# Attention softmax over heads: the layout of the exponentials, the form of their sums and the share of GpSimd are changed

## The chip, the core and the metric

The kernel runs on one core of a Trainium2 chip. The metric is the time of the whole kernel on the device, in microseconds. Before the change the median of 3 runs is 1029.59 us (1028.51 to 1030.99).

## The reference

A gated block of cross attention and a quantised feed-forward net, for 8 sequences of 512 tokens of width 256. Only the attention is touched by the change. Cut to that:

```python
q = (query @ Wq + bq).reshape(Bq, Sq, H, DK)      # Bq = 8, Sq = Sk = 512, H = 16, DK = 16
k = (key @ Wk + bk).reshape(Bq, Sk, H, DK)
v = (value @ Wv + bv).reshape(Bq, Sk, H, DK)
scores = jnp.einsum('bqhd,bkhd->hbqk', q, k) / np.sqrt(DK)
attn = jax.nn.softmax(scores.reshape(H * Bq, Sq, Sk), axis=0).reshape(H, Bq, Sq, Sk)
out = jnp.einsum('hbqk,bkhd->bqhd', attn, v).reshape(Bq, Sq, H * DK)
```

The softmax runs over axis 0, which is heads and batch together: for each pair of a query position and a key position, the 16 x 8 = 128 exponentials of all heads and all sequences are summed, and each is divided by that sum. So no product with v can be scaled afterwards by one factor a query: each exponential is multiplied by its own reciprocal before it meets v.

## The kernel before

Four stages follow each other: `prepare` (projections, stacks of q and k in DRAM), `maxima` (the maximum over heads and batch, `shift`), `attend`, and `ffn`. The change touches `attend` alone.

`attend` runs over 4 query chunks of 128 (`qc`) and for each over 64 steps: 4 key chunks (`kc`) times 16 heads (`h`). A step makes the 128 keys x (8 sequences x 128 queries) exponentials of one head, CT = 1024 for each of the 128 partitions, and stores them in one slot of the ring `e`, as 8 blocks of 128 queries, one for each sequence. 16 steps of one key chunk share one sum. The engines work as follows.

- SyncE loads k for the step four ahead (L653), and for the last 16 steps of a query chunk also q of the next chunk; at step `LAG + 2` of the next chunk it stores the finished sums of the last one (L592, eight transfers), ahead of the further k loads in its queue.
- TensorE (program L683 and on) makes the scores of a step in two halves, each into its own bank `ps` (`shift` subtracted by L694, then four products, L698). The first half of the next step waits for ScalarE to have read the same bank (`exped`). Then it multiplies the scaled exponentials of the step 20 back (`LAG`) with v: `times_v`, L716, eight f32 products with 32 columns each, four column groups of the array side by side, accumulated in `acc` (each is recorded as two instructions). This waits for `pool_scaled` and `dve_scaled` of that step.
- ScalarE takes exp of each half from `ps` into the slot (L763, 512 elements). It waits for the slot to be multiplied already. After each query chunk it copies `acc` out (`gather`, L754), and TensorE waits for that before it clears `acc`.
- VectorE first scales the step 17 back (`SLAG`, L798), the last 2 or 3 of its 8 blocks, with the reciprocals in PSUM (`recip_v`); then it adds the step's two halves to `total`, 512 columns in PSUM (L819 or, for the first head, a copy at L821; then L823). Each add waits for the one before it (`sum_done`). After the 16th head it folds 4 blocks into 128 sums (L826, a reduce over a step of 128 elements), takes the reciprocal into `recip` (L832) and copies it into PSUM (L834).
- GpSimd scales the first 6 or, in one step of 4, 5 blocks of each slot with `recip` (L786). It waits only for `recip_ready`, once in 16 steps. In the very last 16 steps its share is 3 and 2 blocks.

The ring has 21 slots and an extra one for the last step of a query chunk. After the last step, 17 scales of VectorE and 20 `times_v` remain.

Of the kernel before, what the change touches and what calls it, by code (L numbers as in the profile page):

```python
# [595 lines left out]
def attend(nc, sem, k_stack, q_stack, out_parts, ffn_small, x_first, keep):  # L596
# [14 lines left out]
    RING = 21  # L611

    def slot(i):

        i %= STEPS
        return RING if i == STEPS - 1 else i % RING

    def pool_share(i, ending):

        if ending and i >= STEPS - H:  # L620
            return 3 if i < STEPS - H // 2 else 2
        return 6 if i % 4 else 5

    with ExitStack() as es:
        def sb(name, shape, dt=F32):
            return es.enter_context(nc.sbuf_tensor(name, shape, dt))

        e = sb("e", [P, RING + 1, CT])
# [5 lines left out]
        total = es.enter_context(nc.psum_tensor("total", [P, BANK], F32))  # L634
# [5 lines left out]
                                       "recip_copied", "pool_scaled", "dve_scaled", "multiplied", "gathered"))  # L640

        with nc.Block() as block:
# [40 lines left out]
            def _(pe):  # L683
# [22 lines left out]
                def times_v(done, i, half):  # L706

                    kc, h = i // H, i % H
                    if half == 0:
                        pe.wait_ge(pool_scaled, done)  # L710
                        pe.wait_ge(dve_scaled, done)
                    for b in range(half * HB, (half + 1) * HB):
# [4 lines left out]
                                                e[:, slot(i), b * P:(b + 1) * P], start=False, stop=False,  # L717
# [13 lines left out]
                def chunk(qc, first):  # L731
                    for i in range(STEPS):
# [7 lines left out]
                        if i >= LAG or not first:  # L740
                            for half in range(2):
                                times_v(qc * STEPS + (i - LAG + 1), (i - LAG) % STEPS, half)
# [3 lines left out]
                for i in range(STEPS - LAG, STEPS):  # L746
                    for half in range(2):
                        times_v((NC - 1) * STEPS + i + 1, i, half)

            @block.scalar  # L750
            def _(act):
# [4 lines left out]
                def chunk(qc, first):  # L756
                    for i in range(STEPS):
# [3 lines left out]
                        for half in range(2):  # L761
                            act.wait_ge(scored, qc * (2 * STEPS) + (2 * i + half + 1))
                            nc.scalar.activation(e[:, slot(i), half * BANK:(half + 1) * BANK], ps[half][:], ACT.Exp,  # L763
                                                 scale=DK ** -0.5).then_inc(exped, 1)
# [10 lines left out]
            def _(pool):  # L775
# [3 lines left out]
                def chunk(qc, ending):  # L779
                    for i in range(STEPS):  # L780
                        kc = i // H
                        if i % H == 0:
                            pool.wait_ge(recip_ready, qc * NC + (kc + 1))
                        share = pool_share(i, ending)
                        part = e[:, slot(i), 0:share * P].rearrange("p (b q) -> p b q", q=P)
                        nc.gpsimd.tensor_tensor(part, part, recip[:, kc % 2, :].rearrange("p (a q) -> p a q", a=1)  # L786
                                                .to_broadcast([P, share, P]), ALU.mult).then_inc(pool_scaled, 1)
# [5 lines left out]
            def _(dve):  # L793
                def scale(i, ending=False):
                    kc = (i // H) % NC
                    share = pool_share(i % STEPS, ending)
# [585 lines left out]
```

## Time and profile before

| | us |
|---|---|
| median of 3 runs | 1029.59 |
| the profiled execution | 1029.23 |
| its span, first to last instruction | 1027.3 |
| VectorE busy | 897.1 (87%) |
| TensorE busy | 797.8 (78%) |
| ScalarE busy | 645.1 (63%) |
| GpSimd busy | 519.2 (51%) |
| first and last exponential start | 357.5 and 819.7 |

The profile is one execution on the chip. PE is TensorE (PEld its weight loads), DVE is VectorE, ACT is ScalarE, POOL is GpSimd, SP is SyncE; L12 is line 12 of the kernel. A group or a timeline row names engine, line, operation, and output <- inputs. Behind a row stands the idle time of the engine just before it, and what released it. In a timeline, instructions that follow each other closely are merged into one piece, which carries the shape of only one of them; their starts tell the pace better than their durations, since neighbours overlap. The granted clock PEclk is a share of TensorE's full 2.4 GHz.

### The profile page before, as it was taken

To read this page: it belongs to the slowest core of one execution; us is meant where nothing else is said; L and a number is where in the kernel's file an instruction comes from. 1 tells how busy PE (TensorE), PEld (TensorE's weight loads), DVE (VectorE), ACT (ScalarE), POOL (GpSimd) and SP (SyncE) were. 2 spreads that over 40 slices of the span, in tenths; PEclk is the share of its full clock that TensorE was granted. 3 is DMA by queue.
4 is the path that set the end of the run, shared out by engine and by line. 5 is a ranking of instruction groups with operands and counts; after the bars stand their busy time and mean duration, and the time that the engine had idled before them with its cause. 6 is when DMAs were issued, how large, how long until landed. Compare 5 with 4: busy or idle time off the path is not lost. (4 is left out here: it accounts for less than half of the span.)

```text
span 1027.3 us, 21516 instructions
## 1 busy us (share of the span) xinstructions
PE 797.8 (78%) x8175; PEld 445.5 (43%) x8184; DVE 897.1 (87%) x1428; ACT 645.1 (63%) x981; POOL 519.2 (51%) x330
## 2 busy tenths in 40 slices
PE   2798883777777689989888998988889869067656
PEld 1455540111111145555555655655556548022223
DVE  3679843999999889999989999999989978868968
ACT  3354562999999776655655656655656502567673
POOL 4132330000000009999989999999989976022300
PEclk9898896999999899999999999999999979589979
DMA  9489897455445665586556846576465446000013
GB/s 283 164 266 347 262 332 266 164 196 210 167 176 209 229 185 153 145 265 183 148 168 192 279 143 170 158 233 215 138 176 164 129 171 190 0 1 1 0 42 123
DMA packets 112396, 180.94 MB, mean 176 GB/s; under 512 B 10032, under 2 KB 37296, under 8 KB 112304
## 3 DMA queue, kind: packets, MB, share of 16 engines
q1 hardware_dynamic: 112304, 179.67, 55.0%
q8 instruction: 63, 1.03, 0.4%
q14 instruction: 29, 0.24, 0.1%
HBM read 137.70 MB, written 41.94 MB: 175 GB/s over the span
## 5 line engine op out<-in xcount | busy, mean ns | idle before, releaser
L786 POOL TENSOR_TENSOR e<-e,recip 128x768 f32<-128x768 f32 (+3 forms) x256 | 424.7, 1712 | 59.8 <-DVE recip L832 59.8
L763 ACT ACTIVATE e<-ps_att 128x512 f32<-128x512 f32 x512 | 279.6, 595 | 172.4 <-PE ps_att L698 171.9
L694 PE MATMUL ps_att<-shift,minus 128*128 128x512 bf16 x512 | 201.6, 394 | 20.3 <-DMA arena<-k_stack 8.9
L698 PE MATMUL ps_att<-arena 128*128 128x128 bf16 x2048 | 203.4, 223 | 0.0
L716 PE MATMUL acc<-e,arena 128*32 128x128 f32 x4096 | 170.6, 285 | 37.9 <-DVE e L798 33.8
L553 ACT ACTIVATE copies<-ps_max 128x1024 bf16<-128x1024 f32 x192 | 179.0, 1031 | 20.9 <-PE ps_max L533 20.9
L698 PEld LDWEIGHTS ps_att<-arena 128*128 128x128 bf16 x2048 | 161.6, 100 | 64.0 <-issue 6.0
L823 DVE TENSOR_TENSOR total<-total,e 128x512 f32<-128x512 f32 x256 | 178.9, 699 | 8.7
L533 PE MATMUL ps_max<-q_head,k_head 128*128 128x512 bf16 x512 | 138.4, 386 | 60.7 <-DVE high L572 21.5
L819 DVE TENSOR_TENSOR total<-total,e 128x512 f32<-128x512 f32 x240 | 166.3, 693 | 2.1 <-ACT e L763 0.7
L716 PEld LDWEIGHTS acc<-e,arena 128*32 128x32 f32 x4096 | 105.2, 111 | 74.5 <-issue 54.0
L798 DVE TENSOR_TENSOR e<-e,recip_v 128x256 f32<-128x256 f32 (+3 forms) x256 | 119.0, 470 | 4.2 <-ACT e L763 4.2
L577 DVE TENSOR_TENSOR high<-copies,high 128x3072 bf16<-128x3072 bf16 x64 | 111.6, 1744 | 0.0
L533 PEld LDWEIGHTS ps_max<-q_head,k_head 128*128 128x128 bf16 x512 | 34.8, 97 | 164.0 <-ACT copies L553 72.6
L50 POOL MEMSET minus<- 128x128 bf16 x1 | 0.2, 206 | 204.1 <-POOLq L498 204.1
L572 DVE TENSOR_TENSOR high<-ps_max,high 128x1024 bf16<-128x1024 f32 x64 | 77.6, 1212 | 7.5 <-PE ps_max L533 7.5
L191 POOL TENSOR_TENSOR parts<-rest,parts 128x512 bf16<-128x512 f32 x32 | 37.2, 1163 | 91.1 <-ACT parts L321 91.1
L694 PEld LDWEIGHTS ps_att<-shift,minus 128*128 128x128 bf16 x512 | 50.1, 98 | 72.4 <-issue 54.6
L455 DVE TENSOR_TENSOR rest<-full,parts 128x512 f32<-128x512 f32 x32 | 32.8, 1023 | 27.1 <-ACT parts L347 27.1
L216 PE MATMUL psT<-ident,arena 128*128 128x128 f32 x128 | 23.4, 323 | 32.2 <-POOL ident L52 12.3
L1180 POOL TENSOR_TENSOR arena<-up,sil 128x512 f32<-128x512 f32 x16 | 21.6, 1350 | 50.8 <-ACT up L1114 50.8
L1285 PE MATMUL psD<-wd_T,hq 128*128 128x256 bf16 x192 | 30.0, 288 | 20.6 <-DVE hq L1263 20.6
(129 smaller groups left out, 850.8 us busy)
## 6 DMA issues: line engine op xcount, KB each, us to landing
arena<-k_stack SPq DMA_DIRECT2D x256, 256.0 KB, 2.9
k_stack<-parts SPq DMA_DIRECT2D x64, 256.0 KB, 3.8
q_stack<-parts SPq DMA_DIRECT2D x64, 256.0 KB, 3.7
k_head<-k_stack SPq DMA_DIRECT2D x16, 1024.0 KB, 5.6
q_head<-q_stack SPq DMA_DIRECT2D x16, 1024.0 KB, 7.8
arena<-q_stack SPq DMA_DIRECT2D x64, 256.0 KB, 4.4
arena<-in_x_dram SPq DMA_DIRECT2D x5, 1024.0 KB, 7.8
arena<-in_ctx_dram SPq DMA_DIRECT2D x4, 1024.0 KB, 6.9
```

Of the source, the lines that this page charges most:

```text
L533: last = nc.tensor.matmul(ps[:, kc, j * S:(j + 1) * S], k_head[:, i, kc, b * P:(b + 1) * P], q_head[:, i].rearrange("p c (b q) -> p c b q" ...
L553: nc.scalar.activation(copies[:, bp % RING, kc, :], ps[:, kc, :], ACT.Copy).then_inc(copied, 1)
L572: nc.vector.tensor_tensor(high[:, COPIED, :], ps[:, COPIED, :], high[:, COPIED, :], ALU.max).then_inc(updated, 1)
L577: nc.vector.tensor_tensor(high[:, 0:COPIED, :], copies[:, bp % RING], high[:, 0:COPIED, :], ALU.max).then_inc(updated, 1)
L694: nc.tensor.matmul(ps[half][:], minus[:], shift_at(qc, kc).to_broadcast([P, HB, P]), start=True, stop=False, skip_group_check=True)
L698: last = nc.tensor.matmul(ps[half][:, j * P:(j + 1) * P], ks[:, i % KRING, b * P:(b + 1) * P], qs[:, h, b * P:(b + 1) * P], start=False, s ...
L716: last = nc.tensor.matmul(acc[grp:grp + 32, col:col + P], vpad[:, kc, b, v_col:v_col + 32], e[:, slot(i), b * P:(b + 1) * P], start=False, ...
L763: nc.scalar.activation(e[:, slot(i), half * BANK:(half + 1) * BANK], ps[half][:], ACT.Exp, scale=DK ** -0.5).then_inc(exped, 1)
L786: nc.gpsimd.tensor_tensor(part, part, recip[:, kc % 2, :].rearrange("p (a q) -> p a q", a=1) .to_broadcast([P, share, P]), ALU.mult).then_ ...
L798: nc.vector.tensor_tensor(part, part, recip_v[:, (kc % 2) * P:(kc % 2 + 1) * P] .rearrange("p (a q) -> p a q", a=1).to_broadcast([P, B - s ...
L819: nc.vector.tensor_tensor(total[:], total[:], e[:, slot(i), 0:BANK], ALU.add).then_inc(sum_done, 1)
L823: nc.vector.tensor_tensor(total[:], total[:], e[:, slot(i), BANK:CT], ALU.add).then_inc(sum_done, 1)
```

## The change

The ring `e` is laid out anew. Two steps (an even one and the odd one behind it) share a region of 2048 elements in a partition, ordered by query pair (64), step of the two, sequence (8), query within the pair (2). Two neighbouring queries of one sequence and step stay next to each other (8 bytes); the next pair of the same sequence and step lies 128 bytes on. `e_at` gives the view of some blocks of a step. ScalarE's exp writes that way, TensorE's `times_v` and both scales read that way; `by_pairs` gives the reciprocals the matching order. The ring has 22 slots, and the extra slot is gone.

The sums are made anew. VectorE adds nothing in the even steps. In the odd ones it waits for the exponentials of both, and one `tensor_reduce` over step and sequence (16 values, 8 bytes apart) turns the 2048 elements into 128 partial sums, in `pair_sums` (8 x 128 f32, in SBUF). After 16 steps another reduce folds the 8 partial sums, 1024 elements, into `summed`. `total` in PSUM is gone. VectorE's wait for the exponentials now stands behind the scale of that step.

GpSimd scales 6 blocks in odd steps and 5 in even ones, 5.5 on average in place of 5.75, and VectorE the rest. The shares of the last 16 steps stay.

```diff
@@ -608,36 +608,43 @@
     ALL = NC * STEPS
     LAG = 20
     SLAG = 17
-    RING = 21
-
-    def slot(i):
+    RING = 22
+    PAIRS = H // 2
+    QP = P // 2
+
+    def pool_share(i, ending):
 
         i %= STEPS
-        return RING if i == STEPS - 1 else i % RING
-
-    def pool_share(i, ending):
-
         if ending and i >= STEPS - H:
             return 3 if i < STEPS - H // 2 else 2
-        return 6 if i % 4 else 5
+        return 6 if i % 2 else 5
 
     with ExitStack() as es:
         def sb(name, shape, dt=F32):
             return es.enter_context(nc.sbuf_tensor(name, shape, dt))
 
-        e = sb("e", [P, RING + 1, CT])
+        e = sb("e", [P, RING // 2, QP, 2, B, 2])
+        pair_sums = sb("pair_sums", [P, QP, PAIRS, 2])
...
-        total = es.enter_context(nc.psum_tensor("total", [P, BANK], F32))
         recip_v = es.enter_context(nc.psum_tensor("recip_v", [P, BANK], F32))
         acc = es.enter_context(nc.psum_tensor("acc", [P, 4 * BANK], F32))
 
...
+        def e_at(g, b0, b1):
+
+            slot = g % RING
+            return e[:, slot // 2, :, slot % 2, b0:b1, :]
+
+        def by_pairs(vec, n):
+
+            return vec.rearrange("p (q a i) -> p q a i", a=1, i=2).to_broadcast([P, QP, n, 2])
 
...
-                def times_v(done, i, half):
-
-                    kc, h = i // H, i % H
+                def times_v(g, half):
+
+                    kc, h = g % STEPS // H, g % H
                     if half == 0:
-                        pe.wait_ge(pool_scaled, done)
-                        pe.wait_ge(dve_scaled, done)
+                        pe.wait_ge(pool_scaled, g + 1)
+                        pe.wait_ge(dve_scaled, g + 1)
...
-                                                e[:, slot(i), b * P:(b + 1) * P], start=False, stop=False,
+                                                e_at(g, b, b + 1), start=False, stop=False,
                                                 skip_group_check=True)
...
@@ -760,8 +767,10 @@
                             act.wait_ge(multiplied, qc * STEPS + (i - RING + 1))
                         for half in range(2):
                             act.wait_ge(scored, qc * (2 * STEPS) + (2 * i + half + 1))
-                            nc.scalar.activation(e[:, slot(i), half * BANK:(half + 1) * BANK], ps[half][:], ACT.Exp,
-                                                 scale=DK ** -0.5).then_inc(exped, 1)
+                            nc.scalar.activation(
+                                e_at(qc * STEPS + i, half * HB, (half + 1) * HB).rearrange("p q b i -> p b q i"),
+                                ps[half][:].rearrange("p (b q i) -> p b q i", b=HB, i=2), ACT.Exp,
+                                scale=DK ** -0.5).then_inc(exped, 1)
                         if i == LAG - 1 and not first:
 
                             gather(qc * STEPS)
@@ -782,64 +791,59 @@
                         if i % H == 0:
                             pool.wait_ge(recip_ready, qc * NC + (kc + 1))
                         share = pool_share(i, ending)
-                        part = e[:, slot(i), 0:share * P].rearrange("p (b q) -> p b q", q=P)
-                        nc.gpsimd.tensor_tensor(part, part, recip[:, kc % 2, :].rearrange("p (a q) -> p a q", a=1)
-                                                .to_broadcast([P, share, P]), ALU.mult).then_inc(pool_scaled, 1)
+                        part = e_at(qc * STEPS + i, 0, share)
+                        nc.gpsimd.tensor_tensor(part, part, by_pairs(recip[:, kc % 2, :], share), ALU.mult
+                                                ).then_inc(pool_scaled, 1)
                 for qc in range(NC - 1):
                     chunk(qc, False)
                 chunk(NC - 1, True)
 
             @block.vector
             def _(dve):
-                def scale(i, ending=False):
-                    kc = (i // H) % NC
-                    share = pool_share(i % STEPS, ending)
-                    part = e[:, slot(i), share * P:CT].rearrange("p (b q) -> p b q", q=P)
-                    nc.vector.tensor_tensor(part, part, recip_v[:, (kc % 2) * P:(kc % 2 + 1) * P]
-                                            .rearrange("p (a q) -> p a q", a=1).to_broadcast([P, B - share, P]),
+                def scale(g, ending=False):
+                    kc = g % STEPS // H
+                    share = pool_share(g, ending)
+                    part = e_at(g, share, B)
+                    nc.vector.tensor_tensor(part, part, by_pairs(recip_v[:, (kc % 2) * P:(kc % 2 + 1) * P], B - share),
                                             ALU.mult).then_inc(dve_scaled, 1)
 
-                SUMS = 2 * H + 1
-
-                def chunk(qc, first):
+                SUMS = PAIRS + 1
+
+                def chunk(qc):
                     for i in range(STEPS):
                         kc, h = i // H, i % H
-                        done = qc * (NC * SUMS) + kc * SUMS
-
-                        if i < SLAG and first:
-                            dve.wait_ge(exped, qc * (2 * STEPS) + (2 * i + 2))
-                        else:
+                        g = qc * STEPS + i
+                        region = g // H
+                        if g >= SLAG:
                             if h == SLAG % H:
-                                dve.wait_ge(recip_copied, qc * NC + (i - SLAG + STEPS) // H - NC + 1)
-
-                            dve.wait_ge(exped, qc * (2 * STEPS) + (2 * i + 2))
-                            scale(i - SLAG)
-                        if h:
-                            dve.wait_ge(sum_done, done + 2 * h)
-                            nc.vector.tensor_tensor(total[:], total[:], e[:, slot(i), 0:BANK], ALU.add).then_inc(sum_done, 1)
-                        else:
-                            nc.vector.tensor_copy(total[:], e[:, slot(i), 0:BANK]).then_inc(sum_done, 1)
-                        dve.wait_ge(sum_done, done + (2 * h + 1))
-                        nc.vector.tensor_tensor(total[:], total[:], e[:, slot(i), BANK:CT], ALU.add).then_inc(sum_done, 1)
+                                dve.wait_ge(recip_copied, (g - SLAG) // H + 1)
+                            scale(g - SLAG)
+                        if h % 2 == 0:
+                            continue
+                        dve.wait_ge(exped, 2 * g + 2)
+                        if h == 1 and region:
+                            dve.wait_ge(sum_done, region * SUMS)
+                        nc.vector.tensor_reduce(pair_sums[:, :, h // 2, :],
+                                                e[:, g % RING // 2].rearrange("p q s b i -> p q i (s b)"), AX.X, ALU.add
+                                                ).then_inc(sum_done, 1)
                         if h == H - 1:
-                            dve.wait_ge(sum_done, done + (SUMS - 1))
-                            nc.vector.tensor_reduce(summed[:], total[:].rearrange("p (b q) -> p q b", q=P), AX.X,
-                                                    ALU.add).then_inc(sum_done, 1)
-                            dve.wait_ge(sum_done, done + SUMS)
-                            if not (first and kc < 2):
-
-                                dve.wait_ge(pool_scaled, qc * STEPS + (i + 1 - 2 * H))
+                            dve.wait_ge(sum_done, region * SUMS + PAIRS)
+                            nc.vector.tensor_reduce(summed[:].rearrange("p (q i) -> p q i", i=2),
+                                                    pair_sums[:].rearrange("p q s i -> p q i s"), AX.X, ALU.add
+                                                    ).then_inc(sum_done, 1)
+                            dve.wait_ge(sum_done, (region + 1) * SUMS)
+                            if region >= 2:
+                                dve.wait_ge(pool_scaled, (region - 1) * H)
                             nc.vector.reciprocal(recip[:, kc % 2, :], summed[:]).then_inc(recip_ready, 1)
-                            dve.wait_ge(recip_ready, qc * NC + (kc + 1))
+                            dve.wait_ge(recip_ready, region + 1)
                             nc.vector.tensor_copy(recip_v[:, (kc % 2) * P:(kc % 2 + 1) * P], recip[:, kc % 2, :]
                                                   ).then_inc(recip_copied, 1)
-                chunk(0, True)
-                for qc in range(1, NC):
-                    chunk(qc, False)
-                for i in range(STEPS - SLAG, STEPS):
-                    if i % H == 0:
+                for qc in range(NC):
+                    chunk(qc)
+                for g in range(ALL - SLAG, ALL):
+                    if g % H == 0:
                         dve.wait_ge(recip_copied, NC * NC)
-                    scale(i, ending=True)
+                    scale(g, ending=True)
 
 
 def ffn(nc, sem, x, out_parts, out, keep):
```

## Rows read from the trace of the kernel before

**Rows 1.** Page, part 1: us busy (share of the span), instructions of each engine.

```profile
PE 797.8 (78%) x8175; PEld 445.5 (43%) x8184; DVE 897.1 (87%) x1428; ACT 645.1 (63%) x981; POOL 519.2 (51%) x330
```

**Rows 2.** Windows, 598 to 620: busy per engine, granted clock, DMA share, GB/s.

```profile
598.00:620.00 22.00, 21.62 (x352) 14.05 (x348) 21.52 (x39) 14.80 (x29) 21.44 (x13) 1.00 0.55 164
```

**Rows 3.** Timeline, VectorE, 617 to 622: start us, duration us, what.

```profile
617.64 0.41 DVE L798 TENSOR_TENSOR e<-e,recip_v 128x256 f32<-128x256 f32 x1
617.97 0.69 DVE L819 TENSOR_TENSOR total<-total,e 128x512 f32<-128x512 f32 x1
618.69 0.70 DVE L823 TENSOR_TENSOR total<-total,e 128x512 f32<-128x512 f32 x1
619.43 0.69 DVE L826 TENSOR_REDUCE summed<-total 128x128 f32<-128x512 f32 x1
620.15 0.95 DVE L832 RECIPROCAL recip<-summed 128x128 f32<-128x128 f32 x1
621.14 0.29 DVE L834 COPY recip_v<-recip 128x128 f32<-128x128 f32 x1
621.34 0.41 DVE L798 TENSOR_TENSOR e<-e,recip_v 128x256 f32<-128x256 f32 x1
```

**Rows 4.** Timeline, GpSimd: pieces of 16, with the idle time before.

```profile
385.82 27.44 POOL L786 TENSOR_TENSOR e<-e,recip 128x640 f32<-128x640 f32 x16 [29.43 <-DVE recip L832]
...
533.68 27.45 POOL L786 TENSOR_TENSOR e<-e,recip 128x640 f32<-128x640 f32 x16 [4.16 <-DVE recip L832]
...
592.02 27.43 POOL L786 TENSOR_TENSOR e<-e,recip 128x640 f32<-128x640 f32 x16 [1.73 <-DVE recip L832]
621.18 27.43 POOL L786 TENSOR_TENSOR e<-e,recip 128x640 f32<-128x640 f32 x16 [1.74 <-DVE recip L832]
...
827.63 13.30 POOL L786 TENSOR_TENSOR e<-e,recip 128x384 f32<-128x384 f32 x16 [1.75 <-DVE recip L832]
```

**Rows 5.** Groups by shape: scales on both engines; count, busy us, mean ns.

```profile
L786 POOL TENSOR_TENSOR e<-e,recip 128x768 f32<-128x768 f32 x180 | 323.8, 1838 | 0.0
...
L786 POOL TENSOR_TENSOR e<-e,recip 128x640 f32<-128x640 f32 x60 | 93.6, 1560 | 58.1 <-DVE recip L832 58.1
...
L798 DVE TENSOR_TENSOR e<-e,recip_v 128x256 f32<-128x256 f32 x180 | 73.7, 409 | 4.2 <-ACT e L763 4.2
...
L798 DVE TENSOR_TENSOR e<-e,recip_v 128x384 f32<-128x384 f32 x60 | 32.6, 543 | 0.0
```

**Rows 6.** Groups by shape: reduces of VectorE elsewhere.

```profile
L1138 DVE TENSOR_REDUCE hmax<-arena 128x1 f32<-128x1024 f32 x24 | 28.8, 1202 | 0.0
...
L423 DVE TENSOR_REDUCE w_max<-arena 128x2 f32<-128x1408 f32 x1 | 1.6, 1604 | 0.0
```

**Rows 7.** Timeline, TensorE, two steps near 646: times_v, then the scores.

```profile
646.09 0.64 PE L716 MATMUL acc<-e,arena 128*32 128x128 f32 x16
646.66 0.39 PE L694 MATMUL ps_att<-shift,minus 128*128 128x512 bf16 x1
...
647.65 0.64 PE L716 MATMUL acc<-e,arena 128*32 128x128 f32 x16
```

**Rows 8.** Timeline, ScalarE: pairs of exps and the gather.

```profile
379.06 1.08 ACT L763 ACTIVATE e<-ps_att 128x512 f32<-128x512 f32 x2 [0.29 <-PE ps_att L698]
...
598.75 1.08 ACT L763 ACTIVATE e<-ps_att 128x512 f32<-128x512 f32 x2 [0.58 <-PE ps_att L698]
...
622.60 1.88 ACT L754 ACTIVATE arena<-acc 128x2048 f32<-128x2048 f32 x1 [2.03 <-PE acc L716]
...
626.79 1.08 ACT L763 ACTIVATE e<-ps_att 128x512 f32<-128x512 f32 x2 [1.34 <-PE ps_att L698]
```

**Rows 9.** Groups by shape: ScalarE reading 64 bytes apart (L326) and dense (L347).

```profile
L347 ACT ACTIVATE parts<-full 128x512 bf16<-128x512 f32 x32 | 19.7, 616 | 0.0
...
L326 ACT ACTIVATE wk_p<-wk_s 128x512 f32<-128x512 f32 x1 | 1.1, 1068 | 11.8 <-DMA bv_s<-in_L_xattn_bv_dram 11.8
```

**Rows 10.** Waits, 400 to 800 us: waited for, total us, times, longest.

```profile
PE ps_att L694 <- DMA arena<-k_stack: 8.9, 3, 3.6
```

More of the change, by code:

```diff
@@ L741, in chunk @@
                             for half in range(2):
-                                times_v(qc * STEPS + (i - LAG + 1), (i - LAG) % STEPS, half)
+                                times_v(qc * STEPS + i - LAG, half)
                 chunk(0, True)
@@ L745, in _ @@
                     chunk(qc, False)
-                for i in range(STEPS - LAG, STEPS):
+                for g in range(ALL - LAG, ALL):
                     for half in range(2):
-                        times_v((NC - 1) * STEPS + i + 1, i, half)
+                        times_v(g, half)
             @block.scalar
```

## The prediction

> **What bounds the kernel now.** I read the busy time by engine first: VectorE 87% of the span and GpSimd 51%, which averages over stages with different limits [rows 1]. Only the attention stage changes (from 356 to 842 us), so next comes a window inside it, where nothing special happens: in 22 us VectorE works 21.52, GpSimd 21.44, TensorE 21.62 and ScalarE 14.80 [rows 2]. Three engines look full, and the timelines tell which one really sets the pace. The unit of order is what I call a region: 16 steps (one key chunk, 16 heads) that end in one reciprocal. GpSimd's timeline has one piece for each: it starts at the reciprocal, works 27.43 us, then idles 1.74 us for VectorE's next reciprocal [rows 4]. So GpSimd is not the bound. TensorE repeats its step (times_v 0.57 us, then the scores) every 1.56 us where it isn't held [rows 7], 16 x 1.56 = 25.0 a region. VectorE is full: scale, add, add at starts 617.64, 617.97, 618.69, and the next instruction at 619.43, so a scale of two blocks takes 0.33 from start to start, the first add 0.72, the second 0.61 when an independent scale follows and 0.74 when a dependent one does [rows 3]. That is 1.66 a step. A scale of three blocks is 0.13 longer (543 against 409 ns [rows 5]), in 4 of 16 steps: 12 x 1.66 + 4 x 1.79 = 27.1. The end of a region adds 0.13 (the dependent add), 0.72 (reduce), 0.99 (reciprocal) and 0.20 (copy) [rows 3]: 2.04. Together 29.1 us, and the distance of two GpSimd pieces is 621.18 - 592.02 = 29.16 [rows 4]. **VectorE is the bound**, by 1.7 us a region over GpSimd and 4.1 over TensorE.
>
> From the first recip to the last one it is 827.63 - 385.82 = 441.8 us for 15 regions, 29.45 each [rows 4]; the 0.3 over 29.16 is two regions of 31.5 (piece 533.68 has 4.16 of idle time in place of 1.74). There TensorE waited for k_stack, 8.9 us in three waits, 3.6 the longest [rows 10], of which 2 x 2.4 came through.
>
> **VectorE, sums.** For two steps the change takes away four adds (or a copy and three adds) and puts one tensor_reduce of 2048 elements. The trace has reduces from SBUF of 1024 (1202 ns) and 1408 (1604 ns) elements [rows 6], a slope of 1.05 ns an element; 2048 is 1604 + 640 x 1.05 = 2.27 us, or 2.18 from start to start with an independent scale behind it (the add loses the same 0.09). Both rows read neighbouring elements, and the new one reads every second (8 bytes apart). The lower bound is therefore 2.27. For the upper one the nearest row is a ScalarE copy of 512 elements read at 64 bytes a step: 1068 ns, against 616 for a dense one [rows 9], 0.88 ns more an element; 2048 of them would make 4.07 us. Between them lies the old fold, which reads PSUM 512 bytes apart at the dense price (0.69 us for 512 elements, at 619.43 [rows 3]), though from the other memory. I take 2.27: it is VectorE's own row, and 8 bytes are nearer to dense than to 64.
> The Trainium skill speaks against the change here: VectorE: DVE Perf Modes, Rules for kernel authors, calls tensor_reduce the slowest operation, to be restructured on a hot path. The rows disagree for f32: 1024 elements reduced take 1.20 us [rows 6], two adds of 512 take 0.69 + 0.70 [rows 3]; by the rule the sums gain nothing and the time stays near 1029, by the rows the two adds of a step (1.33 from start to start) become half a reduce (1.09).
>
> **VectorE, scales.** GpSimd's share falls from 5.75 to 5.5 blocks, VectorE's rises from 2.25 to 2.5: per two steps one scale of 0.33 and one of 0.46 [rows 3, 5]. A pair of steps then costs 2.18 + 0.33 + 0.46 = 2.97 where it was 3.39 on average (27.1 / 8).
>
> **VectorE, end of a region.** The last reduce isn't followed by an independent instruction (+0.12), the fold reads 1024 values in place of 512: 1.23 in place of 0.72 [rows 6]; reciprocal and copy stay, 0.99 + 0.20. Sum 2.54. A region: 8 x 2.97 + 2.54 = **26.3 us**, against 29.1.
>
> **GpSimd.** Pieces of 12 x 1.838 + 4 x 1.560 = 28.3 by durations took 27.43 [rows 4, 5], so each start overlaps its predecessor by 0.06. Now it is 8 of each: 8 x (1.78 + 1.50) = **26.3 us**, a tie with VectorE; it may not idle at all any more. The inner run of its operands falls from 128 elements to 2 for the reciprocals. No row shows that; bounds are minus 2% (its own spread) and, with half the elements paying the 0.88 of [rows 9], +0.34 us on 768 elements. I take nothing, since consecutive pairs of e are still 12 elements in a row.
>
> **ScalarE.** The exp writes pairs at 128-byte steps. Two exps take 1.08 now [rows 8], and the region 16 x 1.08 = 17.3. With half the elements paying 0.88 it is 0.82 an exp and 1.54 a step: still hidden under the 1.64 of VectorE. With all paying, 1.05 and 1.9 a step: 30.4, the bound. I take nothing; the cover is 9 us.
>
> **TensorE.** times_v streams pairs out of e. 25.0 us a region if unchanged, cover 1.3; its 0.57 us [rows 7] may become 1.14. I take 0, for this stream is a slow one: its eight blocks of 128 elements take 0.57 us with four column groups side by side, so each group spends 0.29 us on a block (2.2 ns an element), while the scores pass 2048 columns in 0.99 us (0.5 ns) [rows 7]. A jump of 0.88 ns on every second element would fit in between.
> Trainium skill, Advanced Engine Details and Errata, Memory Cachelines: SBUF reads at full rate if at least two accesses fall into one line of 16 bytes. Each new pattern has two (pairs of 4 bytes, or steps of 8), and the 64-byte row [rows 9] has one, so trace and rule agree as far as this goes, and by it none of these costs would exist; it bears on the chances only.
>
> **Waits.** DVE's wait on exped moves behind the scale of that step, and comes once in two steps: behind it are queued only the reduce and later scales. The ring is read by the same counts with one more slot; it held nothing before. No queue of SP or GpSimd gets another instruction, and the k loads stay.
>
> **What is late next.** The tie makes stalls visible that VectorE's length hid. After the reciprocal that releases GpSimd at 592.02 [rows 4] ScalarE does the fifth and sixth step of the region with pauses, and from the seventh, at 598.75 [rows 8], its steps follow TensorE's 1.56 [rows 7]: the sixteenth ends 6.8 + 9 x 1.56 + 1.1 = 21.9 us after the reciprocal. VectorE wants it at 26.3 less the last reduce, the fold and the reciprocal: 26.3 - 4.5 = 21.8. No cover is left there, where VectorE had 29.2 - 3.2 - 21.9 = 4.1 us before. So the regions with the gather (ScalarE's 1.88 us copy from 622.60; its sixth step is at 626.79, the rest every 1.56 [rows 8], so the sixteenth ends 5.6 + 10 x 1.56 + 1.1 = 22.3 after the reciprocal) lose about 0.6 each, three times; the k waits come through whole, 8.9; and I add 0.1 a region for hand-overs between engines that now take turns as the last one (GpSimd starts 0.08 after the reciprocal's end, 621.18 against 620.15 + 0.95 [rows 3, 4]). 15 x 26.4 + 1.8 + 8.9 = 406.7 in place of 441.8: -35.1 us. That is with TensorE at full clock, as in the window (1.00 [rows 2]).
> Up to the first reciprocal: the 16th pair of exps ends at 380.15 [rows 8]; then 2.27 + 1.23 + 0.95 gives 384.7 against 385.7: -1.0. After the last one 16 steps are scaled with the old shares, 13.3 us [rows 4]: 0. Sum -36.1, on the profiled execution's 1029.2 (span 1027.3 and 1.9 around it): 993.1, and the median of the runs is 0.4 over that execution: **993.5 us**. Its own range: with stalls as hidden as now 15 x 26.3 + 4.7 = 399, 985; with a few per cent on either side of the reduce and of GpSimd, 980 to 1005.
>
> **Rivals.** (a) Part of it only: GpSimd's short runs cost 4 to 8%, a region of 27.3 to 28.4, 13 to 30 us over the forecast, or stalls of the three nearly equal engines add 1 us or more a region: 1006 to 1025. For it speaks that GpSimd's idle time is only 1.7 us and its cover is gone. (b) GpSimd pays the +0.34 (0.28 on 640): 8 x (2.12 + 1.78) = 31.2 a region, 15 x 1.75 = 26 more than now: 1055. It decides from 12% (29.4 / 26.3) on. (c) The slower end: VectorE's reduce at 8-byte steps. It pays half of 0.88 on each element: 3.17 us, region 26.3 + 8 x 0.90 + 0.4 = 33.9, 15 x 4.5 = +67: 1097; paying all, 1220. It decides where the reduce takes over 2.66 us (2.27 + 3.15 / 8). Against it: the fold of PSUM at 512 bytes a step isn't dear [rows 3]. (d) ScalarE's writes pay all: 30.4 and a quarter of the gather's 1.88, 30.9, 15 x 1.45 = 22 more, and 8 us before the first reciprocal: 1059. Decides above 1.0 us an exp. (e) TensorE's times_v doubles: 16 x 2.13 = 34.1: 1100; decides above 0.86 us. (f) It doesn't do what it says (GpSimd and VectorE merely swap who waits): 1027 to 1031.
>
> **Chances.** Forecast 0.57, (a) 0.14, (f) 0.03, (b) 0.08, (c) 0.08, (d) 0.05, (e) 0.05. Range 980 to 1056: it leaves out (c), (e), (d) and a little on either side of the rest. Faster by over 0.2% (what a measurement of this kernel can tell): 0.71; within it: 0.03; slower: 0.26.
>
> **What would show it.** Right: reduces of 2048 at 2.27 us, folds at 1.2, exps at 0.60, GpSimd forms at 1.84 and 1.56, reciprocals 26.4 to 27.5 apart, GpSimd without idle time, TensorE's step still 1.56. Wrong: any of these dearer in its own row, or reciprocals further apart than the longest engine's sum, which would mean a loop of waits that I don't see.

## The result, and the profile after

The changed kernel takes 996.0 us (median of 4 runs, 995.64 to 999.43), against 1029.05 for the kernel before (4 runs): a ratio of 0.970, 95% interval 0.967 to 0.972. The profiled execution took 996.3, its span is 994.4. The prediction was 993.5, in a range of 980 to 1056.

The page after: busy time by engine, then the groups of the attention stage (columns as in [rows 5]; `L826` is the reduce of 2048, `L831` the fold, `L723` times_v, `L807` and `L795` the scales of VectorE and GpSimd).

```profile
PE 793.8 (80%) x8184; PEld 443.8 (45%) x8184; DVE 869.2 (87%) x1044; ACT 674.1 (68%) x981; POOL 442.5 (44%) x330
```

```profile
L770 ACT ACTIVATE e<-ps_att 128x512 f32<-128x512 f32 x512 | 308.7, 666 | 116.1 <-PE ps_att L705 116.0
L826 DVE TENSOR_REDUCE pair_sums<-e 128x128 f32<-128x2048 f32 x128 | 292.1, 2282 | 19.5 <-ACT e L770 18.8
...
L795 POOL TENSOR_TENSOR e<-e,recip 128x768 f32<-128x768 f32 x120 | 186.4, 1553 | 0.0
L723 PE MATMUL acc<-e,arena 128*32 128x128 f32 x4096 | 179.6, 295 | 10.9 <-DVE e L807 10.4 <-issue 0.3 <-POOL e L795 0.2
...
L795 POOL TENSOR_TENSOR e<-e,recip 128x640 f32<-128x640 f32 x120 | 160.0, 1333 | 97.4 <-DVE recip L837 97.4
...
L807 DVE TENSOR_TENSOR e<-e,recip_v 128x384 f32<-128x384 f32 x120 | 65.8, 549 | 0.0
...
L807 DVE TENSOR_TENSOR e<-e,recip_v 128x256 f32<-128x256 f32 x120 | 49.2, 410 | 0.0
...
L831 DVE TENSOR_REDUCE summed<-pair_sums 128x128 f32<-128x1024 f32 x16 | 19.5, 1221 | 0.5
```

Against [rows 5] two things stand out. The reduce of 2048 takes 2.28 us, as its neighbours in [rows 6] said. And GpSimd's 768 elements take 1.55 us where they took 1.84, 640 take 1.33 where they took 1.56, which nothing in the prediction expected. ScalarE's exps went the other way, from 0.60 us to 0.67.

The timeline of VectorE around a reciprocal, the answer to [rows 3]:

```profile
562.65 0.88 DVE L807 TENSOR_TENSOR e<-e,recip_v 128x256 f32<-128x256 f32 x2
563.44 2.27 DVE L826 TENSOR_REDUCE pair_sums<-e 128x128 f32<-128x2048 f32 x1
565.64 0.87 DVE L807 TENSOR_TENSOR e<-e,recip_v 128x256 f32<-128x256 f32 x2
566.43 2.27 DVE L826 TENSOR_REDUCE pair_sums<-e 128x128 f32<-128x2048 f32 x1
568.74 1.22 DVE L831 TENSOR_REDUCE summed<-pair_sums 128x128 f32<-128x1024 f32 x1
570.00 0.95 DVE L837 RECIPROCAL recip<-summed 128x128 f32<-128x128 f32 x1
570.99 0.29 DVE L839 COPY recip_v<-recip 128x128 f32<-128x128 f32 x1
571.19 0.88 DVE L807 TENSOR_TENSOR e<-e,recip_v 128x256 f32<-128x256 f32 x2
```

Two scales, then a reduce: 2.99 from 562.65 to 565.64, where 2.97 was forecast. The fold takes 1.26 from start to start, the reciprocal 0.99, the copy 0.20. VectorE is still without a gap.

The timeline of GpSimd, the answer to [rows 4], with an ordinary region and the three long ones:

```profile
383.28 22.42 POOL L795 TENSOR_TENSOR e<-e,recip 128x640 f32<-128x640 f32 x16 [28.90 <-DVE recip L837]
409.58 22.42 POOL L795 TENSOR_TENSOR e<-e,recip 128x640 f32<-128x640 f32 x16 [3.87 <-DVE recip L837]
...
489.05 22.28 POOL L795 TENSOR_TENSOR e<-e,recip 128x640 f32<-128x640 f32 x16 [4.07 <-DVE recip L837]
518.05 22.44 POOL L795 TENSOR_TENSOR e<-e,recip 128x640 f32<-128x640 f32 x16 [6.72 <-DVE recip L837]
...
597.51 22.30 POOL L795 TENSOR_TENSOR e<-e,recip 128x640 f32<-128x640 f32 x16 [4.05 <-DVE recip L837]
628.91 22.45 POOL L795 TENSOR_TENSOR e<-e,recip 128x640 f32<-128x640 f32 x16 [9.10 <-DVE recip L837]
...
708.38 22.34 POOL L795 TENSOR_TENSOR e<-e,recip 128x640 f32<-128x640 f32 x16 [4.04 <-DVE recip L837]
738.98 22.45 POOL L795 TENSOR_TENSOR e<-e,recip 128x640 f32<-128x640 f32 x16 [8.25 <-DVE recip L837]
...
791.96 11.94 POOL L795 TENSOR_TENSOR e<-e,recip 128x384 f32<-128x384 f32 x16 [4.03 <-DVE recip L837]
```

Its piece is 22.43 us now and not 26.3, and it idles 4.05 in each region, more than before. From the first reciprocal to the last it is 791.96 - 383.28 = 408.7 us, against 441.8: -33.1. Twelve regions are 26.5 long (first one 26.3), three are 29.0, 31.4 and 30.6.

TensorE, the answer to [rows 7]:

```profile
576.65 0.70 PE L723 MATMUL acc<-e,arena 128*32 128x128 f32 x16
577.28 0.39 PE L701 MATMUL ps_att<-shift,minus 128*128 128x512 bf16 x1
...
578.27 0.70 PE L723 MATMUL acc<-e,arena 128*32 128x128 f32 x16
```

A step is 578.27 - 576.65 = 1.62, with times_v 0.63 of it (0.57 before); 16 steps are 25.9 us.

The three long regions are those with a gather, and TensorE waits for k in each: 1.3, 2.1 and 2.8 us. In the second, of 31.4 us, its clock falls as well:

```profile
609.99 0.69 PE L723 MATMUL acc<-e,arena 128*32 128x128 f32 x16
612.78 0.61 PE L701 MATMUL ps_att<-shift,minus 128*128 128x512 bf16 x1 [2.11 <-DMA arena<-k_stack]
...
615.61 0.61 PE L701 MATMUL ps_att<-shift,minus 128*128 128x512 bf16 x1
...
617.51 0.39 PE L701 MATMUL ps_att<-shift,minus 128*128 128x512 bf16 x1
```

```profile
597.50:628.80 31.30, 27.82 (x415) 17.40 (x413) 26.79 (x27) 20.75 (x33) 22.30 (x16) 0.95 0.59 167
```

The granted clock is 0.95 over this region, and 0.50 (1.2 GHz) from 614 to 616. The step that starts at 612.78 takes 2.83 us and the next one 1.90, where 1.62 is usual: 1.5 us more. In the third long region two waits for k, of 1.5 and 1.3 us, left the clock at 1.00. With 1.2 us a time for the gather (from an experiment below) the parts are 1.2 + 1.3, 1.2 + 2.1 + 1.5 and 1.2 + 2.8, against 2.5, 4.9 and 4.1 us over an ordinary region.

**Where the 32.9 us of span went.** The time between first and last reciprocal is 33.1 shorter. From the first exponential (355.53, before 357.54) to the first reciprocal it is 0.5 shorter. What remains is in stages that the change doesn't touch: the attention started 2.0 earlier, and from the last reciprocal to the end it is 202.4 in place of 199.7. I put these two down to scatter between executions: in the second profile of the same kernel (below, median 992.75) the end took 199.5, and between the reciprocals it was 406.3.

### The profile page after: what moved, and what is told of

It reads as the page before. It is cut to its first block and busy times, and to the rows that moved or that the text cites. A ratio compares the mean times of both kernels' runs of the same rounds, so it can differ in the third digit from the quotient of the medians.

```text
span 994.4 us, 21125 instructions
## 1 busy us (share of the span) xinstructions
PE 793.8 (80%) x8184; PEld 443.8 (45%) x8184; DVE 869.2 (87%) x1044; ACT 674.1 (68%) x981; POOL 442.5 (44%) x330
## 5 line engine op out<-in xcount | busy, mean ns | idle before, releaser
L795 POOL TENSOR_TENSOR e<-e,recip 128x640 f32<-128x640 f32 (+3 forms) x256 | 348.1, 1403 | 101.4 <-DVE recip L837 101.4
L770 ACT ACTIVATE e<-ps_att 128x512 f32<-128x512 f32 x512 | 308.7, 666 | 116.1 <-PE ps_att L705 116.0
L826 DVE TENSOR_REDUCE pair_sums<-e 128x128 f32<-128x2048 f32 x128 | 292.1, 2282 | 19.5 <-ACT e L770 18.8
L701 PE MATMUL ps_att<-shift,minus 128*128 128x512 bf16 x512 | 199.1, 389 | 18.4 <-DMA arena<-k_stack 6.6
L705 PE MATMUL ps_att<-arena 128*128 128x128 bf16 x2048 | 200.1, 221 | 0.0
L723 PE MATMUL acc<-e,arena 128*32 128x128 f32 x4096 | 179.6, 295 | 10.9 <-DVE e L807 10.4
L705 PEld LDWEIGHTS ps_att<-arena 128*128 128x128 bf16 x2048 | 159.1, 99 | 62.0 <-issue 2.7
L723 PEld LDWEIGHTS acc<-e,arena 128*32 128x32 f32 x4096 | 107.1, 111 | 40.4 <-issue 13.4
L807 DVE TENSOR_TENSOR e<-e,recip_v 128x384 f32<-128x384 f32 (+3 forms) x256 | 118.0, 505 | 0.0
L1112 ACT ACTIVATE sil<-psG,gscale 128x512 f32<-128x512 f32 (+1 forms) x48 | 33.1, 690 | 20.8 <-PE psU L1215 17.0
```

Of the source, the lines that this page charges most:

```text
L701: nc.tensor.matmul(ps[half][:], minus[:], shift_at(qc, kc).to_broadcast([P, HB, P]), start=True, stop=False, skip_group_check=True)
L705: last = nc.tensor.matmul(ps[half][:, j * P:(j + 1) * P], ks[:, i % KRING, b * P:(b + 1) * P], qs[:, h, b * P:(b + 1) * P], start=False, s ...
L723: last = nc.tensor.matmul(acc[grp:grp + 32, col:col + P], vpad[:, kc, b, v_col:v_col + 32], e_at(g, b, b + 1), start=False, stop=False, sk ...
L770: nc.scalar.activation(e_at(qc * STEPS + i, half * HB, (half + 1) * HB).rearrange("p q b i -> p b q i"), ps[half][:].rearrange("p (b q i) ...
L795: nc.gpsimd.tensor_tensor(part, part, by_pairs(recip[:, kc % 2, :], share), ALU.mult).then_inc(pool_scaled, 1)
L807: nc.vector.tensor_tensor(part, part, by_pairs(recip_v[:, (kc % 2) * P:(kc % 2 + 1) * P], B - share), ALU.mult).then_inc(dve_scaled, 1)
```

## The experiments

The theory: the time is VectorE's, which is still the engine without a gap; the sums give the gain, and the layout is there to make the sums cheap. What I had to test besides is why GpSimd became 15% faster, and what the layout costs the others.

**The layout alone.** The adds and the shares of before, with VectorE's wait ahead of the scale as before, on the new ring:

```diff
-        nc.vector.tensor_reduce(pair_sums[:, :, h // 2, :], e[:, g % RING // 2].rearrange("p q s b i -> p q i (s b)"), ...)
+        total_v = total[:].rearrange("p (q b i) -> p q b i", b=HB, i=2)
+        nc.vector.tensor_tensor(total_v, total_v, e_at(g, 0, HB), ALU.add)
+        nc.vector.tensor_tensor(total_v, total_v, e_at(g, HB, B), ALU.add)
```

> The new layout of e alone: the adds into total (four in two steps) and the shares (6, 6, 6, 5 blocks) of before stay. Theory (the gain is that of VectorE's sums): VectorE's region is still 12 x 1.66 + 4 x 1.79 + 2.04 = 29.1 us, reciprocals 29.2 apart, 1029 us within 5. Rival (the gain is that of the layout, by GpSimd's 15% or otherwise): reciprocals under 28 us apart, 1010 us or less. On GpSimd: if its 1.55 us for 768 elements comes from the layout, it shows 1.55 here too; if it comes from VectorE's reduces beside it in place of adds, it shows 1.84. On ScalarE: if the exp's 0.67 us comes from writing pairs 128 bytes apart, 0.67 here.

Measured: 1026.1 us, ratio 0.999 (0.996 to 1.002). Its groups:

```profile
L770 ACT ACTIVATE e<-ps_att 128x512 f32<-128x512 f32 x512 | 301.8, 653 | 148.3 <-PE ps_att L705 147.9
L795 POOL TENSOR_TENSOR e<-e,recip 128x768 f32<-128x768 f32 x180 | 273.3, 1548 | 0.0
...
L829 DVE TENSOR_TENSOR total<-total,e 128x512 f32<-128x512 f32 x256 | 178.9, 699 | 8.7
```

and two pieces of GpSimd's timeline:

```profile
587.99 23.17 POOL L795 TENSOR_TENSOR e<-e,recip 128x640 f32<-128x640 f32 x16 [5.91 <-DVE recip L838]
617.15 23.11 POOL L795 TENSOR_TENSOR e<-e,recip 128x640 f32<-128x640 f32 x16 [6.00 <-DVE recip L838]
```

The reciprocals are 29.16 apart, to the hundredth as before, and GpSimd waits 6 us in each region. So the layout gives nothing by itself; GpSimd's speed comes with it (1.55 us beside the old adds), and so does ScalarE's loss (0.65).

**The sums alone**, over the old layout and with the shares of before, two whole slots read by one reduce; all other reads and writes of e go block by block again:

```diff
-        e = sb("e", [P, RING // 2, QP, 2, B, 2])
+        e = sb("e", [P, RING, CT])
-        ... e[:, g % RING // 2].rearrange("p q s b i -> p q i (s b)")
+        ... e[:, g % RING - 1:g % RING + 1, :].rearrange("p s (b q i) -> p q i (s b)", b=B, i=2)
```

> The new sums alone, over the old layout: e has 22 whole slots, one tensor_reduce over two of them reads 512 bytes a step; the shares are 6, 6, 6, 5. Theory (the layout is there for the reduce; far steps cost VectorE up to 0.88 ns an element as they cost ScalarE): the reduce takes 4.0 us, a region 8 x (3.95 + 0.33 + 0.36) + 2.5 = 39.6 us, 1190 us. Rival (a far step costs VectorE nothing, as in its fold of PSUM): 2.28 us, reciprocals 26 to 27.5 apart, 990 to 1005 us, and the layout would be needless. GpSimd's 768 elements: 1.84 if the layout made it faster, 1.55 if the reduces beside it did.

Measured: 1158.4 us, ratio 1.126 (1.118 to 1.134).

```profile
L824 DVE TENSOR_REDUCE pair_sums<-e 128x128 f32<-128x2048 f32 x128 | 479.6, 3752 | 5.5 <-ACT e L769 5.5
L793 POOL TENSOR_TENSOR e<-e,recip 128x768 f32<-128x768 f32 x180 | 323.0, 1826 | 0.0
L769 ACT ACTIVATE e<-ps_att 128x512 f32<-128x512 f32 x512 | 280.1, 595 | 292.9 <-PE ps_att L704 292.3
```

The reduce takes 3.75 us in place of 2.28, 0.72 ns more an element; the theory had taken 0.88 from ScalarE. Reciprocals come 37.7 apart. GpSimd is back at 1.83 and the exps at 0.60, so both come with the layout and neither with VectorE's reduces (for GpSimd, the walk below tells what in it). The same kind of step costs VectorE nothing in PSUM (the old fold, [rows 3]); in SBUF it does.

**Single queries in place of pairs**, 4 bytes every 64, the reduce reading 16 neighbours:

```diff
-        e = sb("e", [P, RING // 2, QP, 2, B, 2])
+        e = sb("e", [P, RING // 2, P, 2, B])
```

> The changed kernel with e ordered by single queries: 4 bytes, the next query of the same sequence 64 bytes on; the reduce reads 16 neighbours. Theory (a lone element costs up to 0.88 ns more wherever it is read or written, a pair little): exps at 1.0 to 1.05 us and a ScalarE region of 31 us or more, times_v longer than 0.63 us, reduce at 2.28; 1050 us or more. Rival (pairs weren't needed): exps at 0.67, 996 us within 5.

Measured: 1130.8 us, ratio 1.099 (1.092 to 1.107).

```profile
L770 ACT ACTIVATE e<-ps_att 128x512 f32<-128x512 f32 x512 | 515.2, 1116 | 42.3 <-PE ps_att L705 32.0
L826 DVE TENSOR_REDUCE pair_sums<-e 128x128 f32<-128x2048 f32 x128 | 292.8, 2287 | 141.4 <-ACT e L770 140.8
L723 PE MATMUL acc<-e,arena 128*32 128x128 f32 x4096 | 281.6, 408 | 2.9 <-DVE e L807 2.9
...
L795 POOL TENSOR_TENSOR e<-e,recip 128x768 f32<-128x768 f32 x120 | 188.8, 1574 | 0.0
```

```profile
641.87 1.11 PE L723 MATMUL acc<-e,arena 128*32 128x128 f32 x16
642.92 0.39 PE L701 MATMUL ps_att<-shift,minus 128*128 128x512 bf16 x1
```

```profile
DVE pair_sums L826 <- ACT e L770: 112.9, 89, 3.4
```

The exp takes 1.12 us (1.0 ns more an element than the 0.60 of before), times_v 1.05 (641.87 to 642.92), and VectorE, with the same 2.29 us for a reduce, now waits 113 us for ScalarE. Reciprocals are 35.1 apart. TensorE is as full as ScalarE here (79.1 and 74.1 of the 80 us from 400 on), and the two wait for each other in short turns, so the run doesn't tell how much of the lost time is the exp's and how much is times_v's. The reduce gains nothing from neighbours over 8-byte steps, and everything else loses: that is what the pairs are for. Memory Cachelines (the Trainium skill, Advanced Engine Details and Errata) promises full rate for at least two accesses to a line of 16 bytes, and a penalty for one. The runs agree on the penalty, for ScalarE's writes too. Full rate holds for VectorE's reduce; for the exps (0.67 in place of 0.60) and times_v (0.63 in place of 0.57) it holds only nearly.

**GpSimd's walk alone**, in the kernel before:

```diff
-  part = e[:, slot(i), 0:share * P].rearrange("p (b q) -> p b q", q=P)
-  ... recip[:, kc % 2, :].rearrange("p (a q) -> p a q", a=1).to_broadcast([P, share, P])
+  part = e[:, slot(i), 0:share * P].rearrange("p (b q i) -> p q b i", b=share, i=2)
+  ... recip[:, kc % 2, :].rearrange("p (q a i) -> p q a i", a=1, i=2).to_broadcast([P, P // 2, share, 2])
```

> The kernel before; only GpSimd walks its blocks by query pair (pair, sequence, query in the pair) over the old layout, each pair 512 bytes from the next of its walk. Theory (GpSimd's speed is in the order of its walk: the reciprocals come as one pair repeated): 768 elements at 1.55 us or less, time as before. Rival (it is in the placement, 12 or 10 neighbours in a row): 1.84 or more; above 2.0 us GpSimd would become the bound and the time rises over 1040.

```profile
L786 POOL TENSOR_TENSOR e<-e,recip 128x768 f32<-128x768 f32 x180 | 272.6, 1546 | 0.0
...
L786 POOL TENSOR_TENSOR e<-e,recip 128x640 f32<-128x640 f32 x60 | 79.7, 1328 | 116.1 <-DVE recip L832 116.1
```

1029.0 us in its one run, and 1.55 us for 768 elements over the old placement, whose pairs lie 512 bytes apart along the walk. So it is the order of the walk (one pair of queries through all sequences, then the next pair) and not the placement of e. GpSimd waits 6 us a region in this kernel and the time stays: room, and no gain by itself. The walk changes for e and for the reciprocals at once, and no run tells which of the two is cheaper for it, or why.

**Who sets the pace now.** The changed kernel itself ran again beside three variants, on one chip.

> The changed kernel as it is, beside the next three on the same chip: 996 us within 4, reciprocals 26.5 apart, three gaps of 29 to 31.5.

> The changed kernel with GpSimd at 6 blocks in every step. Theory (VectorE is still the bound, TensorE right behind it at 16 x 1.62 = 25.9): VectorE loses 8 x 0.13 = 1.1 us a region, 25.4, so TensorE takes over and the reciprocals come 25.9 to 26.0 apart, 7 to 9 us less. Rival 1 (TensorE's 25.9 isn't a bound): 25.4 apart, 16 us less. Rival 2 (GpSimd is the bound in spite of its idle time): longer by 16 x 0.11 a region, 27 us more.

> The changed kernel with GpSimd at 5 blocks in every step, so VectorE scales 3. Theory (VectorE is the bound): +8 x 0.13 = 1.07 us a region, reciprocals 27.5 to 27.6 apart, 16 us more. Rival (TensorE or ScalarE is the bound at 26.5): no change.

> The changed kernel with the eight stores of a query chunk issued one a step, each between two loads of k, in place of all eight ahead of the next load. Theory (the three long gaps, 11.5 us over 26.5 in all, come from loads of k queued behind the stores): TensorE's waits for k_stack shrink to under 0.5 us, the gaps to 27 to 27.5, 8 to 10 us less. Rival (they come from the gather of acc, or from the q loads of the steps before): no change.

The edits of the first two are one line:

```diff
-        return 6 if i % 2 else 5
+        return 6                      # the other: return 5
```

and of the third, in SyncE's program:

```diff
-                        if i == LAG + 2 and not first:
-                            store(qc - 1)
+                        if LAG + 2 <= i < LAG + 2 + B and not first:
+                            store(qc - 1, i - LAG - 2)      # one of the eight transfers
```

| | median us | ratio (95%) | first to last reciprocal | ordinary regions | the three long ones |
|---|---|---|---|---|---|
| changed kernel | 992.75 | 0.965 (0.961 to 0.969) | 406.3 | 26.5 | 29.1, 29.4, 30.1 |
| GpSimd 6 blocks | 989.53 | 0.962 (0.957 to 0.966) | 401.2 | 25.6 to 26.0 | 30.0, 31.7, 29.4 |
| GpSimd 5 blocks | 1008.13 | 0.978 (0.973 to 0.983) | 421.5 | 27.55 | 31.2, 29.8, 30.1 |
| stores spread | 989.61 | 0.964 (0.957 to 0.970) | 400.8 | 26.5 | 27.7, 27.8, 27.7 |

With 5 blocks the ordinary region grows by 1.07 and the time by 15.4 us: the theory's 16, and VectorE is the bound. With 6 blocks it shrinks by 0.6 and not by 1.07, to TensorE's 25.9; TensorE is busy 79.9 of the 80 us from 400 on, where it was 78.6 in the kernel beside it. The waits of that kernel show the change of hands; VectorE now waits 31 times for exps:

```profile
DVE pair_sums L826 <- ACT e L770: 17.7, 31, 4.1
```

The gain of 3.2 us in the median is less than half of what was expected, since the long regions kept or grew their length (13.5 us over the ordinary ones, 9.1 in the kernel beside it). Part of that is the clock: in the region of 31.7 it fell to 0.52 from 614 to 616, behind a wait for k of 2.3 us, while the kernel beside it kept 1.00 between the reciprocals. That the rest comes from TensorE being full, so that nothing makes up for a stall, is my reading; the next kernel, whose clock didn't fall, bears it out. Spreading the stores takes 5.5 us from the long regions and leaves 1.2 each. That I call the price of the gather, since in each of them TensorE waits 1.0 us for ScalarE's copy of acc and for no k that shows. The waits for k_stack, kernel after and stores spread:

```profile
PEld ps_att L701 <- DMA arena<-k_stack: 7.8, 6, 2.4
```

```profile
PEld ps_att L702 <- DMA arena<-k_stack: 1.0, 3, 0.5
```

The medians of the stores-spread and of the 6-block kernel each lie 3 us below the changed kernel's, and their intervals overlap with its; it is the traces, one of each, that tell them apart. The expected 8 to 10 us was read off the first profile after, whose three gaps (11.5 us in excess) were wider than those of the kernel beside it (9.1): 0.8 us of waits for k and the 1.5 us of the lower clock, which this one did not have.

**Both edits together.**

> The changed kernel with both edits: stores one a step, GpSimd at 6 blocks in every step. Theory (the two gains add, since one is in the three regions with a gather and the other in the twelve others, where TensorE's 25.9 sets the pace): 12 x 25.9 + 3 x 27.3 = 393 us between first and last reciprocal, 13 less than the changed kernel beside it, 979 to 982 us. Rival (TensorE, now without spare time, can't make up the gather, so the long gaps grow as they shrank): 986 us or more.

984.9 us (981.96 to 987.89), ratio 0.958 (0.956 to 0.961), and under the changed kernel's 992.75, which was not run beside it (the kernel before had the same median both times, 1028.4). Between first and last reciprocal 394.7 us, where 393 was expected; the ordinary regions are 25.6 to 26.0, the long ones 27.8 to 28.4. The expectation had 27.3 for these, where the stores-spread kernel already had 27.7, and they grew by 0.2 to 0.7 us each while the ordinary ones shrank by 0.6: 6.9 us over the ordinary ones in all, against 3.6. That is the rival's mechanism, at a small price. The median is 3 us over what was expected, while the profiled execution was 981.96.

**The cheap alternative**: the kernel before, with GpSimd's walk by pairs and 6 and 7 blocks by turns.

```diff
-        return 6 if i % 4 else 5
+        return 6 + i % 2
```

> The kernel before, with its layout and its adds; GpSimd walks by query pair and takes 6 and 7 blocks by turns, VectorE 2 and 1. Theory (VectorE sets the pace, GpSimd's cheaper walk is room that can be traded): VectorE 8 x (1.66 + 1.53) + 2.04 = 27.5 us a region, GpSimd 8 x (1.50 + 1.72) = 25.8: reciprocals 27.6 apart, 1.6 x 15 = 24 us less than before, 1005 us. Rival (GpSimd's walk is dearer at 7 blocks, or the releases of TensorE come later and it becomes the last): 28.5 or more apart, 1018 us or more.

```profile
L786 POOL TENSOR_TENSOR e<-e,recip 128x896 f32<-128x896 f32 x120 | 211.3, 1761 | 0.0
...
L786 POOL TENSOR_TENSOR e<-e,recip 128x768 f32<-128x768 f32 x120 | 185.3, 1544 | 60.8 <-DVE recip L832 60.8
...
L798 DVE TENSOR_TENSOR e<-e,recip_v 128x128 f32<-128x128 f32 x120 | 33.3, 277 | 2.9 <-ACT e L763 2.9
```

1008.3 us, ratio 0.981 (0.978 to 0.984). The ordinary regions are 27.57, the 27.6 expected; the long ones 31.25, 29.3 and 28.0 add what the sum left out (in the first two the clock fell to 0.50). More than half of the change's gain is to be had without a new layout or new sums, by a faster walk that makes room on the engine next to the bound.

## Why the prediction was right, point by point

- **VectorE is the bound, and the region is the sum of its instructions.** Right: 26.3 forecast, 26.49 measured. The 5-block kernel (27.55) shows that it is a bound and not a coincidence.
- **The reduce of 2048 at 2.27 us.** Right (2.28), and the fold at 1.22. The advice against tensor_reduce (the Trainium skill, VectorE: DVE Perf Modes, Rules for kernel authors) did not hold for this f32 sum: one reduce of 2048 takes 2.20 from start to start (563.44 to 565.64), the four adds of 512 took 2.66. The upper end was real, though: with steps of 512 bytes it is 3.75. The price taken from ScalarE's row, 0.88 ns an element, was 0.72 on VectorE.
- **GpSimd at 26.3, a tie with VectorE.** Wrong: 22.4. "I take nothing" was asked in the right place and bounded on the wrong side; the range of minus 2% to +18% held only a loss, and the truth was minus 15%. It did not move the time, because GpSimd was never the last. Rivals (a) and (b) rested on its short runs; they cost nothing. The 0.1 us a region for hand-overs between the two tied engines came out in size and not in cause: GpSimd idled 4 us a region, and the 26.49 over 26.3 is in VectorE's own starts, 8 x 0.02 for two scales and a reduce and 0.03 for the fold. That term was luck.
- **ScalarE and TensorE at no extra cost.** The choice of 0 was wrong in both rows, though small: 0.67 us an exp in place of 0.60, times_v 0.63 in place of 0.57. The first is hidden, as the cover said. The second lifts TensorE's region from 25.0 to 25.9, which cuts its distance from the bound to 0.6: not yet visible, but it is what stops the 6-block kernel. The argument that times_v is too slow a stream to feel the steps failed: it lost 0.06 in pairs and 0.48 with lone elements.
- **Stalls become visible.** Right in size: 12.2 forecast over 15 x 26.3 (1.5, 1.8 and 8.9), 14.2 measured (408.7 - 394.5). The split was off: the gather costs 1.2 a time (stores spread) where 0.6 was forecast, TensorE's waits for k in the long regions came to 6.1 where 8.9 was forecast, the ordinary regions took 2.7 over 26.3 where 1.5 was, and 1.5 is the lower clock, which the prediction put at full. These misses cancel. The kernel before had such falls as well, six between its reciprocals (granted clock 0.50 from 520 to 522, for one); four of them lie in regions of 29.16 or 29.17 and cost nothing, and two in its long regions, so the 2 x 2.4 read there as waits for k alone may hold some of the clock too.
- **First reciprocal 1.0 earlier, end unchanged.** 0.5 earlier against the first exponential; the same gap from the last reciprocal to the next stage (17.2).
- **The sum.** 406.7 between the reciprocals against 408.7 and, in the second profile of the same kernel, 406.3. Errors of parts were off the path (GpSimd), small, or of opposite sign (gather and clock against waits for k). Three sums beside the forecast are off in themselves: 8 x (1.78 + 1.50) is 26.2; exps that all pay 0.88 ns make 1.08 + 0.90 = 1.98 us a step and 31.7 a region, so rival (d) belongs at 1079 and not at 1059; and rival (c), paying all, at about 1212.

Rival (c) was right about its mechanism for steps of 512 bytes, and (d) and (e) for lone elements; pairs stay clear of both.

## What to carry to other kernels

Sum the instructions of the engine without gaps from start to start, and the period comes out within 1%; then ask what the next engine's sum is, since it caps every further gain (25.9 here, 0.6 under the bound). When data is interleaved to please one engine, keep two f32 neighbours together and price every reader and writer of the tile. An operand that is broadcast may be cheap or dear by the order in which it is walked, with no data moved: try that before a new layout.

## What was not expected of the hardware

- GpSimd's tensor_tensor of 768 f32 elements takes 1.84 us when it walks block by block through 128 reciprocals, and 1.55 when each pair of reciprocals serves all blocks before the next pair, wherever the data lies.
- VectorE reads SBUF at 8-byte steps for nothing (2.28 us for 2048, as for neighbours: 2.29) and at 512-byte steps for 0.72 ns an element more.
- ScalarE writes pairs at 128-byte steps almost for nothing while no engine scales, before the first reciprocal, and dearer afterwards; two exps of the kernel after in either stretch (ScalarE's timeline):

```profile
376.13 1.11 ACT L770 ACTIVATE e<-ps_att 128x512 f32<-128x512 f32 x2 [0.30 <-PE ps_att L705]
```

```profile
578.00 1.27 ACT L770 ACTIVATE e<-ps_att 128x512 f32<-128x512 f32 x2 [0.38 <-PE ps_att L705]
```

  That is 1.11 and 1.27 us for two, where the kernel before had 1.08 in both stretches [rows 8]. Over the old layout the exps stay at 0.60 beside the same work of VectorE and GpSimd's walk by pairs (the run of that walk alone), so it takes both, the pairs and busy neighbours; that they compete for SBUF is my reading and not shown. Lone elements cost 1.12 an exp.
- A wait of TensorE of 2.1 us was followed by a granted clock of 0.50 and two slow steps (1.5 us more); waits of 1.3 and 1.5 us in the same trace were not. In the traces of the kernel after, the layout alone, GpSimd's walk alone, 6 blocks, 5 blocks and the cheap alternative one region each is longer than 31 us, and each of the six holds such a fall behind a wait for k.
- TensorE's f32 blocks, four column groups at a time, take 0.57 us dense, 0.63 in pairs, 1.05 alone: eight-byte pieces are nearly, but not wholly, free there.
